# One held element's down projection moved from the end of the kernel into the next element's steps

## The chip, the core and the metric

The kernel runs on one core of a Trainium2 chip. The metric is the device time of one execution in microseconds (us); the median of three runs of the kernel before is 1217.96 us (1217.88 to 1219.26).

## The reference

A transformer block over x of 16 batch elements x 256 positions x 512 channels (f32): a WKV recurrence over the positions of each element, gated and added, then a feed-forward layer that is the sum of a routed part (8 experts, top 2, capacity 1280 rows, inner width 352) and a shared MLP (inner width 1408), gated and added.

```python
x = x + tanh(g_xattn[0]) * wkv(time_decay, time_first, layernorm(x), ctx_2048)
xf = layernorm(x).reshape(4096, 512)
gu = xf @ shared_w_up_gate                      # 512 x 2816
shared = (silu(gu[:, :1408]) * gu[:, 1408:]) @ shared_w_down      # 1408 x 512
logits = xf @ router                            # top 2 of 8, softmax of the two
h = silu(gate) * up                             # per expert, up to 1280 rows, 512 -> 2 x 352
routed = scatter_add(weight * (h @ w_down))     # 352 -> 512
x = x + tanh(g_ffn[0]) * (routed + shared)
```

## The kernel before

**Units and tiles.** One batch element is a unit (u, 0 to 15), made of two tiles of 128 rows (t, 0 and 1; tile number 2u + t). The array `acc` keeps the running sum x of the tiles in SBUF. Every engine has a program of its own, written out in order; semaphores with constant or counted values join them. Each unit is cut into 11 steps (s), one per block of 128 of the shared MLP's 1408 inner columns, and in each step each engine does its part of the MLP for this unit, plus stages of the recurrence and normalization for units to come, at places set by the table `STAGE_AT` (an offset of steps for each of a unit's two tiles). Of those, the stages `divide`, `turn_y`, `add_y`, `norm_x2`, `split_x` and `logits` follow each other from DVE over PE, DVE, ACT and DVE; `split_x` is followed by SyncE's transposing DMA into `xT` (L470), which the `logits` and the next unit's up projection read.

**The shared MLP in f16 halves.** Each f32 operand is split into a high and a low f16 part, and each product is three matmuls. In step s of unit u PE runs `up_pair` (L1060 to L1083), 24 matmuls of 256 columns into PSUM `PU`; ACT takes the silu and the high part, DVE the product (L1373), GpSimd (POOL) the low part (L690). The stages `logits` and `turn_y` are called in the middle of `up_pair`, behind its 9th and 18th matmul. Behind step s of unit u, PE runs `down_block(u - 1, s - 1)` (L1104 to L1116): for both tiles of the unit before, 3 matmuls of 512 columns each, into PSUM `PD[0]` and `PD[1]`, accumulated over the 11 blocks; the last step has two blocks. DVE adds the result into `acc` in step 0 of unit u + 1 (`add_down`, L1426 to L1429). SyncE then stores the finished tiles of units 0 to 12 into the DRAM array `moe_d` (`start_sums`).

**Held units.** Units 13, 14 and 15 (HELD = 3) get no down blocks in the steps: `if s > 0 and not (u.fixed and not 1 <= u.v <= FIRST_HELD)` (L1151), with FIRST_HELD = 13, stops them after unit 13's steps, which carry unit 12's blocks. Their hidden values stay in `hreg`, in three buffers. `held_down(u, t)` (L1214 to L1225) does one tile of a unit, a half, in one piece: 11 blocks x 3 = 33 matmuls of 512 columns. Half (13, 0) runs between unit 15 and the first expert, while the routed rows are gathered; the other five run behind the last expert.

**The experts.** 71 tiles of 128 routed rows (NPOS). For each, POOL gathers the rows from DRAM and SyncE transposes them; PE runs `expert_up` (24 matmuls of 352 columns), `turn_hidden` (3 transposes) and `expert_down` (9 matmuls of 512 columns into `PD[t % 2]`, L1202 to L1212); ACT, DVE and ACT again handle the hidden values and stage the output; POOL adds it into `moe_d` with an accumulating indirect DMA (L809).

**The end.** When the last of these has landed (`rows_added`), SyncE loads the routed sums of the held tiles, 1.5 MB, from `moe_d` (L576), starts two DRAM to DRAM copies of 3328 KB each, `moe_d` to the output, for units 0 to 12 (L578), and then stores the six held tiles from `acc`, 256 KB each (L583), each as soon as its down projection has been added and the routed sums of all six tiles are in (`combined`). DVE adds the six sums (L1626) and then the held halves that are left, in order:

```python
for c in range(FIRST_HELD * UT, TILES):
    sp.wait_ge(combined, HTILES)
    sp.wait_ge(down_added, c + 1)
    sp.dma_start(out_rows[c * P:(c + 1) * P, :], acc[:, c * D:(c + 1) * D]).then_inc(out_stored, 16)
```

Of the kernel before, what the change touches and what calls it, by code (L numbers as in the profile page):

```python
# [12 lines left out]
TILES = BATCH * STEPS // P  # L13
UNITS = BATCH
UT = STEPS // P
# [12 lines left out]
JT = J // P  # L28
# [5 lines left out]
NPOS = NTOK * TOPK // P + E - 1  # L34
# [16 lines left out]
HELD = 3  # L51
PE_TURNED = 2
SQ = 32
FIRST_HELD = UNITS - HELD
HTILES = HELD * UT
SP_N = 3
LOOP = (1, 6)
FIRST_AT = {
# [118 lines left out]
def build(nc, x, ctx_in, g_x, g_f, t_decay, t_first, router, w_ug, w_dn, s_ug, s_dn, out):  # L177
    es = ExitStack()
    with es:
# [118 lines left out]
        wst += [sUw[:, D * r:D * (r + 1)] for r in range(STAGED)]  # L298
        sums = sUw[:, STAGED * D:(STAGED + HTILES) * D].rearrange("p (j c) -> p j c", j=HTILES)

# [37 lines left out]
        PD = [pb(f"PD{r}", [P, 512]) for r in range(2)]  # L338
        PT = pb("PT", [P, 512])
        PR = pb("PR", [P, 512])  # L340
# [24 lines left out]
        down_ready = sem("down_ready"); down_added = sem("down_added")  # L365
# [33 lines left out]
        combined = sem("combined"); out_stored = sem("out_stored")  # L399
# [11 lines left out]
        EARLY_PARTS = 10 + len(ZERO_AT)  # L411
        assert (HTILES + 4) * P == len(ZERO_AT) * UN
        up_set = [(PU[0], PU[1]), (PU[2], PL)]

        def ring_of(u, m):

            n = JT * u.v + m
            if m >= SP_N:
                return n - SP_N + 1
            if u.fixed and u.v == 0:  # L420
                return None
            return JT * (u.v - 1) + max(q for q in range(JT) if q % SP_N == m) + 1

# [4 lines left out]
        def _(sp):  # L428
# [51 lines left out]
            def clear_rows(n):  # L480
                lo = NTOK - HTILES * P + n * UN
                sp.wait_ge(pmade, PMADE)
# [94 lines left out]
            for lo in range(0, held, held // 2):  # L577
                sp.dma_start(out_rows[lo:lo + held // 2, :].rearrange("(p a) d -> p (a d)", p=P),  # L578
                             moe_d[lo:lo + held // 2, :].rearrange("(p a) d -> p (a d)", p=P)).then_inc(out_stored, 16)
            for c in range(FIRST_HELD * UT, TILES):  # L580
                sp.wait_ge(combined, HTILES)
                sp.wait_ge(down_added, c + 1)
                sp.dma_start(out_rows[c * P:(c + 1) * P, :], acc[:, c * D:(c + 1) * D]).then_inc(out_stored, 16)  # L583
            sp.wait_ge(out_stored, 16 * (2 + HTILES))
            sp.wait_ge(moe_started, 16 * MOE_PARTS)
# [8 lines left out]
        def _(pool):  # L594
# [91 lines left out]
            def hidden_lo(u, m):  # L686
                n = JT * u.v + m
                r = m % SP_N
                pool.wait_ge(hhi_ready, n + 1)
# [129 lines left out]
        def _(act):  # L819
# [63 lines left out]
            def hidden_silu(u, m):  # L883
                n = JT * u.v + m
                r = m % SP_N
                act.wait_ge(up_ready, n + 1)
# [114 lines left out]
        def _(pe):  # L1001
# [99 lines left out]
                pe.matmul(PL[0:1, E:E + NPOS], home_of, Pm, start=True, stop=True).then_inc(homes_turned, 1)  # L1101
                pe.matmul(PL[0:1, E + NPOS:E + 2 * NPOS], one, Pm, start=True, stop=True).then_inc(homes_turned, 1)

            def down_block(u, j):  # L1104

                if u.fixed and u.v == 0:
                    pe.wait_ge(wd_lo, j + 1)
                elif j == 0:
                    pe.wait_ge(down_added, UT * u.v)
                pe.wait_ge(hlo_ready, JT * u.v + j + 1)  # L1110
                for t in range(UT):
                    for a, b in ((0, 0), (0, 1), (1, 0)):
                        mm = pe.matmul(PD[t][:, :], hh[:, u.par, j, a, t * P:(t + 1) * P], sD[:, j, b, :],  # L1113
                                       start=(j == 0 and a + b == 0), stop=(j == JT - 1 and a == 1))
                    if j == JT - 1:
                        mm.then_inc(down_ready, 1)  # L1116

            def unit(u, first=0):
                for s in range(first, JT):
                    for v, k in tiles_at("turn_k", u, s):  # L1120
                        if turned_by_pe(v):
                            turn_k(v, k)

                    def attend():
                        for v, k in tiles_at("turn_v", u, s):
                            if turned_by_pe(v):
                                turn_v(v, k)
                        for v, k in tiles_at("logits", u, s):
                            logits(v, k)
                        if u.fixed and u.v >= UNITS - 2:  # L1130
                            if s == (7 if u.v == UNITS - 2 else 1):
                                positions(LAST[u.par], TILES - 1 + u.par)
                            if u.v == UNITS - 1 and s == 3:
                                count_all()
                            if u.v == UNITS - 1 and s == 5:
                                place_homes()
                        elif u.par == 1 and s == 8 and not (u.fixed and u.v < 0):
                            positions(group_route(u.half), UT * u.v + 3)

                    def attend_late():  # L1140
                        for v, k in tiles_at("turn_y", u, s):
                            turn_y(v, k)

                    if u.fixed and u.v < 0:
                        attend()
                        attend_late()
                    else:
                        if u.fixed and u.v == UNITS - 1 and s == TABLE_AT:
                            turn_table()
                        up_pair(u, s, attend, attend_late)  # L1150
                    if s > 0 and not (u.fixed and not 1 <= u.v <= FIRST_HELD):  # L1151
                        down_block(u.shift(-1), s - 1)
                        if s == JT - 1:
                            down_block(u.shift(-1), s)

            pe.wait_ge(pmade, PMADE)
            pe.wait_ge(tab_in, 32)
# [43 lines left out]

            def expert_down(t, h):  # L1202
                pe.wait_ge(ehlo_ready, t + 1)
                if t >= 2:
                    pe.wait_ge(ostaged, t - 1)
                for m in range(IT):
                    M = IM[m]
                    for a, b in ((0, 0), (0, 1), (1, 0)):
                        mm = pe.matmul(PD[t % 2][:, :], ehT[0:M, t % 2, a, m * P:(m + 1) * P],  # L1209
                                       weights(h, UW + (m * 2 + b) * D, M, D),  # L1210
                                       start=(m == 0 and a + b == 0), stop=(m == IT - 1 and a == 1))
                mm.then_inc(edown_ready, 1)  # L1212

            def held_down(u, t):  # L1214

                PX = (PD, (PT, PR))[u % 2][t]
                if u == UNITS - 1:
                    pe.wait_ge(down_added, UT * (u - 2) + t + 1)
                buf = 2 if u == UNITS - 1 else u % 2
                pe.wait_ge(hlo_ready, JT * (u + 1))  # L1220
                for j in range(JT):
                    for a, b in ((0, 0), (0, 1), (1, 0)):
                        mm = pe.matmul(PX[:, :], hh[:, buf, j, a, t * P:(t + 1) * P], sD[:, j, b, :],  # L1223
                                       start=(j == 0 and a + b == 0), stop=(j == JT - 1 and a == 1))
                mm.then_inc(down_ready, 1)  # L1225

            pe.wait_ge(x2_done, TILES)
            held_down(FIRST_HELD, 0)
            pe.wait_ge(gidx_ready, 3)
            pe.wait_ge(down_added, FIRST_HELD * UT)  # L1230
            pe.wait_ge(homes_ready, 1)
# [7 lines left out]
                h = g  # L1239
            turn_hidden(NPOS - 1)  # L1240
            expert_down(NPOS - 1, h)
            held_down(FIRST_HELD, 1)
            for u in range(FIRST_HELD + 1, UNITS):
                if u % 2 == 0:
                    pe.wait_ge(ostaged, NPOS)
                for t in range(UT):
                    held_down(u, t)

# [2 lines left out]
        def _(dve):  # L1253
            def wait_alone(s, v):


                dve.wait_ge(s, v)
                dve.sem_inc(dve_waits, 1)
# [164 lines left out]
                                                  op0=ALU.subtract, op1=ALU.mult))  # L1423
                dve.tensor_tensor(homes, PL[0:1, E:E + NPOS], no_home, ALU.add).then_inc(homes_ready, 1)

            def add_down(c, t, PX):  # L1426
                dve.wait_ge(down_ready, c + 1)
                dve.scalar_tensor_tensor(out=acc_tile(c), in0=PX[t][:, :], scalar=gates[:, 0:1], in1=acc_tile(c),
                                         op0=ALU.mult, op1=ALU.add).then_inc(down_added, 1)  # L1429

# [179 lines left out]
                dve.tensor_tensor(ehT[:, t % 2, 1, :], PR[:, 0:IT * P], ehT[:, t % 2, 0, :], ALU.subtract).then_inc(ehlo_ready, 1)  # L1610

            for t in range(NPOS + 1):
                if t == 2:
                    add_down(FIRST_HELD * UT, 0, (PT, PR))
                if t >= 1:
                    expert_hidden(t - 1)
                    expert_lo(t - 1)
                for e, q in chunks_at(t):
                    weights_lo(e, q)

            add_down(FIRST_HELD * UT + 1, 1, (PT, PR))
            wait_alone(down_added, FIRST_HELD * UT + 2)
            dve.wait_ge(sums_in, 16)
            for t in range(HTILES):
                c = FIRST_HELD * UT + t
                dve.tensor_tensor(acc_tile(c), sums[:, t], acc_tile(c), ALU.add).then_inc(combined, 1)  # L1626
            dve.wait_ge(combined, HTILES)
            for c in range(FIRST_HELD * UT + 2, TILES):
                add_down(c, c % UT, (PD, (PT, PR))[c // UT % 2])


# [19 lines left out]
```

## Time and profile before

| | us |
|---|---|
| median of 3 runs | 1217.96 |
| lowest, highest run | 1217.88, 1219.26 |
| span of the profiled execution, first to last instruction | 1215.5 |
| PE busy | 1150.4 |
| DVE busy | 701.0 |
| POOL busy | 632.3 |
| ACT busy | 488.7 |

The profiled execution has no device time of its own among the times; its span is 2.5 us below the median of the runs, which is what lies around the first and last instruction. All times below are counted from the first instruction. PE is TensorE's matmul stream, and PEclk the clock granted to it, where 1.00 is 2.4 GHz and 0.50 is 1.2 GHz. A row of the timeline gives the start, the time from the first start to the last end, the engine, line and operation, and in brackets the idle time before it with what ended it.

### The profile page before, as it was taken

The page shows a single profiled execution, that of the slowest core. Times are in us where ns is not written, and L with a number is a line of the kernel's source. Part 1 is how long each engine was busy: PE and PEld are TensorE (multiplying, and loading weights), DVE is VectorE, ACT ScalarE, POOL GpSimd, SP SyncE. Part 2 cuts the span into 40 slices and gives each one's busy share as a digit, 9 for nine tenths or more (in the row PEclk, how much of TensorE's full clock was granted, in tenths as well). Part 3 has the DMA queues.
Part 4 walks back from the last instruction along what each step waited for, and adds up shares of the span by engine and source line. Part 5 has one row for each costly group of instructions (what it writes and reads, how often), then busy time and mean ns, then how long its engine had stood idle before and what let it go on. Part 6 is the DMA issues. An engine that isn't in the chain of part 4 may idle for free.

```text
span 1215.5 us, 26048 instructions
## 1 busy us (share of the span) xinstructions
PE 1150.4 (95%) x8284; PEld 803.5 (66%) x8284; DVE 701.0 (58%) x1385; ACT 488.7 (40%) x901; POOL 632.3 (52%) x754
## 2 busy tenths in 40 slices
PE   1489999999999999999999899999999999999998
PEld 1367777777777777777777677666666666666653
DVE  5878787787787787877878855322232222231112
ACT  5666453443443444435435243333343333333220
POOL 7889447456456456456466642444444444444320
PEclk9989999999999999999999999999999999999999
DMA  8554543333343333433443315999999898988748
GB/s 233 139 141 112 135 88 75 83 87 84 73 94 79 83 82 78 101 81 69 114 99 65 67 48 102 205 174 174 173 172 174 165 178 168 178 161 132 128 58 315
DMA packets 296006, 150.98 MB, mean 124 GB/s; under 512 B 236125, under 2 KB 260725, under 8 KB 295776
## 3 DMA queue, kind: packets, MB, share of 16 engines
q1 hardware_dynamic: 277024, 112.24, 40.5%
q0 software_dynamic: 18048, 37.47, 18.0%
q8 instruction: 51, 0.84, 0.3%
q14 instruction: 51, 0.42, 0.1%
q10 hardware_dynamic: 832, 0.02, 0.0%
HBM read 77.17 MB, written 52.31 MB: 107 GB/s over the span
## 4 chain that ended last, share of the span: by engine, by line
PE 77%; issue 7%; DVE 5%; POOL 3%; ACT 2%; DMA 1%; POOLq 1%; DVEq 0%; ACTq 0%; SPq 0%
PE PU L1080 31%; PE PD L1113 14%; PE PU L1188 12%; PE PD L1209 9%; PE PL L1188 4%; PE PR L1199 1%; PE PT L1004 1%; PE PR L1223 1%; PE PT L1223 1%; PE PD L1223 1%; DVE wkv L1338 1%; DMA moe_d<-wkv,acc 1%; POOL xT L792 1%; POOL slot_d L674 0%; POOLq L802 0%
## 5 line engine op out<-in xcount | busy, mean ns | idle before, releaser
L1080 PE MATMUL PU<-xT,wreg 128*128 128x256 f16 x4224 | 503.1, 276 | 1.9 <-DVE srng L1373 1.9
L1080 PEld LDWEIGHTS PU<-xT,wreg 128*128 128x128 f16 x4224 | 414.1, 99 | 81.7 <-issue 2.5
L809 POOL DMA_INDIRECT moe_d<-wkv,acc x71 | 112.0, 1578 | 215.9 <-ACT wkv L984 209.4
L1188 PE MATMUL PU<-acc,wkv 128*128 x1284 | 214.5, 312 | 0.0
L1113 PE MATMUL PD<-wreg,hreg 128*128 128x512 f16 x858 | 206.4, 379 | 0.0
L1188 PEld LDWEIGHTS PU<-acc,wkv 128*128 128x128 f16 x1284 | 125.2, 98 | 69.3
L1610 DVE TENSOR_TENSOR wkv<-PR,wkv 128x384 f16<-128x384 f32 x71 | 39.6, 557 | 208.0 <-ACT wkv L978 208.0
L1209 PE MATMUL PD<-acc,wkv 128*128 (+1 forms) x639 | 149.6, 379 | 1.5 <-DVE wkv L1610 1.5
L890 ACT ACTIVATE srng<-PU 128x256 f32<-128x256 f32 x176 | 66.8, 379 | 200.4 <-PE PU L1080 153.2
L690 POOL TENSOR_TENSOR hreg<-srng,hreg 128x256 f16<-128x256 f32 x165 | 120.0, 731 | 43.3 <-ACT hreg L906 42.4
L1113 PEld LDWEIGHTS PD<-wreg,hreg 128*128 128x128 f16 x858 | 83.9, 98 | 73.5
L906 ACT ACTIVATE hreg<-srng 128x256 f16<-128x256 f32 x176 | 72.3, 411 | 118.1 <-DVE srng L1373 118.0
L1373 DVE SCALAR_TENSOR_TENSOR srng<-PU,srng 128x256 f32<-128x256 f32 x176 | 73.3, 417 | 62.7 <-ACT srng L890 50.0
L1209 PEld LDWEIGHTS PD<-acc,wkv 128*128 128x128 f16 (+1 forms) x639 | 62.5, 98 | 67.7 <-issue 1.7
L1338 DVE RECIPROCAL wkv<-wkv 128x512 f32<-128x512 f32 x32 | 106.9, 3341 | 0.1
L984 ACT ACTIVATE wkv<-PD,acc 128x512 f32<-128x512 f32 x71 | 48.8, 687 | 106.5 <-PE PD L1209 82.8
L674 POOL DMA_INDIRECT slot_d<-stw,sidx x64 | 68.4, 1069 | 22.2 <-issue 15.5
L974 ACT ACTIVATE wkv<-PU 128x352 f32<-128x352 f32 x71 | 33.0, 465 | 113.3 <-PE PU L1188 61.6
L662 POOL TENSOR_TENSOR wkv<-wkv 128x512 f32<-128x512 f32 x32 | 38.7, 1209 | 69.6 <-DVE wkv L1314 69.5
L1188 PE MATMUL PL<-acc,wkv 128*128 x420 | 68.4, 313 | 0.0
L635 POOL TENSOR_SCALAR ve<-mv 128x1 f32<-128x1 f32 x64 | 14.4, 224 | 100.7 <-DVE mv L1288 97.4
L1004 PE MATMUL PT<-ident,wkv 128*128 128x128 f32 x144 | 26.2, 311 | 37.5 <-ACT wkv L854 26.3
(178 smaller groups left out, 1335.1 us busy)
## 6 DMA issues: line engine op xcount, KB each, us to landing
wreg<-in_L_ffn_w_up_gate SPq DMA_DIRECT2D x48, 176.0 KB, 3.9
acc<-in_x SPq DMA_DIRECT2D x32, 256.0 KB, 3.3
xhl_d<-wkv SPq DMA_DIRECT2D x32, 256.0 KB, 2.4
wkv<-in_ctx SPq DMA_DIRECT2D x112, 64.0 KB, 2.5
k_d<-wkv SPq DMA_DIRECT2D x28, 256.0 KB, 3.4
wkv<-k_d SPq DMA_DIRECT2D x112, 64.0 KB
moe_d<-acc SPq DMA_DIRECT2D x13, 512.0 KB
out<-moe_d SPq DMA_DIRECT2D x2, 3328.0 KB, 21.2
```

Of the source, the lines that this page charges most:

```text
L674: pool.indirect_dma_start(out=slot_d, out_offset=bass.IndirectOffsetOnAxis(ap=sidx[:, 2 * (r.at + t) + k:2 * (r.at + t) + k + 1], axis=0), ...
L690: pool.tensor_tensor(hh[:, u.par, m, 1, :], srng[:, r, :], hh[:, u.par, m, 0, :], ALU.subtract).then_inc(hlo_ready, 1)
L809: pool.indirect_dma_start(out=moe_d, out_offset=bass.IndirectOffsetOnAxis(ap=didx[:, t:t + 1], axis=0), in_=ostage[t % 3], in_offset=None, ...
L890: act.activation(srng[:, r, :], PU[r][:, 0:UN], ACT.Silu, scale=1.0 / WS).then_inc(silu_done, 1)
L906: act.activation(hh[:, buf, m, 0, :], srng[:, r, :], ACT.Copy).then_inc(hhi_ready, 1)
L984: act.activation(ostage[t % 3], PD[t % 2][:, :], ACT.Copy, scale=wslot[:, t:t + 1]).then_inc(ostaged, 1)
L1080: mm = pe.matmul(PU[r][:, gu * UN:(gu + 1) * UN], sU[:, m, gu, a, kt, :], xT[:, u.par, b, kt, :], start=(kt == 0 and a + b == 0), stop=(kt ...
L1113: mm = pe.matmul(PD[t][:, :], hh[:, u.par, j, a, t * P:(t + 1) * P], sD[:, j, b, :], start=(j == 0 and a + b == 0), stop=(j == JT - 1 and ...
L1188: mm = pe.matmul(up_set[t % 2][gu][:, 0:I], xgT[:, t % 4, a, kt, :], weights(h, ((gu * 2 + b) * KT + kt) * I, P, I), start=(kt == 0 and a ...
L1209: mm = pe.matmul(PD[t % 2][:, :], ehT[0:M, t % 2, a, m * P:(m + 1) * P], weights(h, UW + (m * 2 + b) * D, M, D), start=(m == 0 and a + b = ...
L1338: dve.reciprocal(nd[:, 1], nd[:, 1]).then_inc(rcp_done, 1)
L1373: dve.scalar_tensor_tensor(out=srng[:, r, :], in0=PU[r][:, UN:2 * UN], scalar=HS / WS, in1=srng[:, r, :], op0=ALU.mult, op1=ALU.mult).then ...
```

## The change

Unit 13's down projection runs block by block in unit 14's steps, as those of units 0 to 12 do in the units behind them, into both `PD` buffers. Half (14, 0) takes the place of (13, 0) between unit 15 and the first expert; halves (14, 1), (15, 0) and (15, 1) stay for the end, in `PR`, `PT` and `PD[1]`. DVE adds both tiles of unit 13 before the first expert's work, and the first `expert_down` waits for that. Semaphore counts are numbered by the new order, `HELD_ORDER`, and SyncE waits for `combined` once instead of for each store.

```diff
+EARLY_HALVES = (0, 1)
+FRONT = (UNITS - 2, 0)
+ENDING = ((UNITS - 2, 1), (UNITS - 1, 0), (UNITS - 1, 1))
+HELD_ORDER = tuple((UNITS - HELD, t) for t in EARLY_HALVES) + (FRONT,) + ENDING
...
-            for c in range(FIRST_HELD * UT, TILES):
-                sp.wait_ge(combined, HTILES)
-                sp.wait_ge(down_added, c + 1)
+            sp.wait_ge(combined, HTILES)
+            for n, (u, t) in enumerate(HELD_ORDER):
+                c = UT * u + t
+                sp.wait_ge(down_added, FIRST_HELD * UT + n + 1)
                 sp.dma_start(out_rows[c * P:(c + 1) * P, :], acc[:, c * D:(c + 1) * D]).then_inc(out_stored, 16)
...
-            def down_block(u, j):
+            def down_block(u, j, halves=range(UT)):
...
+                    if s > 0 and u.fixed and u.v == FIRST_HELD + 1:
+                        down_block(u.shift(-1), s - 1, EARLY_HALVES)
+                        if s == JT - 1:
+                            down_block(u.shift(-1), s, EARLY_HALVES)
...
             def expert_down(t, h):
                 pe.wait_ge(ehlo_ready, t + 1)
+                if t == 0:
+                    pe.wait_ge(down_added, FIRST_HELD * UT + UT)
...
             def held_down(u, t):
-                PX = (PD, (PT, PR))[u % 2][t]
-                if u == UNITS - 1:
-                    pe.wait_ge(down_added, UT * (u - 2) + t + 1)
+                PX = (PT, PR, PT, PD[1])[HELD_ORDER.index((u, t)) - UT]
+                if (u, t) == ENDING[1]:
+                    pe.wait_ge(down_added, FIRST_HELD * UT + UT + 1)
+                if (u, t) == ENDING[2]:
+                    pe.wait_ge(ostaged, NPOS - 1)
...
-            held_down(FIRST_HELD, 0)
+            held_down(*FRONT)
...
-            held_down(FIRST_HELD, 1)
-            for u in range(FIRST_HELD + 1, UNITS):
-                if u % 2 == 0:
-                    pe.wait_ge(ostaged, NPOS)
-                for t in range(UT):
-                    held_down(u, t)
+            for u, t in ENDING:
+                held_down(u, t)
...
             for t in range(NPOS + 1):
+                if t == 0:
+                    for k in range(UT):
+                        add_down(FIRST_HELD * UT + k, k, PD)
                 if t == 2:
-                    add_down(FIRST_HELD * UT, 0, (PT, PR))
+                    add_down(UT * FRONT[0] + FRONT[1], 0, (PT, PR), FIRST_HELD * UT + UT)
...
-            for c in range(FIRST_HELD * UT + 2, TILES):
-                add_down(c, c % UT, (PD, (PT, PR))[c // UT % 2])
+            for n, (u, t) in enumerate(ENDING):
+                add_down(UT * u + t, n, (PR, PT, PD[1]), FIRST_HELD * UT + UT + 1 + n)
```

The first place is PE's program in unit 14, from step 0 to the middle of step 5. L1080 (after the change L1085) is `up_pair`, L1004 (L1009) a transpose of `turn_y`, L1049 (L1054) the `logits`, L1118 a matmul of `down_block`. Before:

```order
L1080 MATMUL PU0<-xT,wreg 128x256 x18
L1004 MATMUL PT<-ident,wkv 128x128 x4
L1080 MATMUL PU0<-xT,wreg 128x256 x6
L1080 MATMUL PU1<-xT,wreg 128x256 x24
L1080 MATMUL PU2<-xT,wreg 128x256 x24
L1080 MATMUL PU0<-xT,wreg 128x256 x24
L1080 MATMUL PU1<-xT,wreg 128x256 x24
L1080 MATMUL PU2<-xT,wreg 128x256 x9
L1049 MATMUL PL<-rt_w,xT 128x16 x8
```

And of the change, the end of the same stretch, steps 3 and 4 and the first part of 5:

```order
L1085 MATMUL PU0<-xT,wreg 128x256 x24
L1118 MATMUL PD0<-wreg,hreg 128x512 x3
L1118 MATMUL PD1<-wreg,hreg 128x512 x3
L1085 MATMUL PU1<-xT,wreg 128x256 x24
L1118 MATMUL PD0<-wreg,hreg 128x512 x3
L1118 MATMUL PD1<-wreg,hreg 128x512 x3
L1085 MATMUL PU2<-xT,wreg 128x256 x9
L1054 MATMUL PL<-rt_w,xT 128x16 x8
```

Behind each of the steps 1 to 9 now stand six matmuls of 512 columns, and twelve behind step 10; four such blocks stand ahead of the `logits` of step 5.

The second place is the end of PE's program, behind the last `expert_down` (L1209, after the change L1220). Before, `held_down` is L1223:

```order
L1209 MATMUL PD0<-acc,wkv 128x512 x2
L1223 MATMUL PR<-wreg,hreg 128x512 x33
L1223 MATMUL PD0<-wreg,hreg 128x512 x33
L1223 MATMUL PD1<-wreg,hreg 128x512 x33
L1223 MATMUL PT<-wreg,hreg 128x512 x33
L1223 MATMUL PR<-wreg,hreg 128x512 x33
```

And of the change, where it is L1236:

```order
L1220 MATMUL PD0<-acc,wkv 128x512 x2
L1236 MATMUL PR<-wreg,hreg 128x512 x33
L1236 MATMUL PT<-wreg,hreg 128x512 x33
L1236 MATMUL PD1<-wreg,hreg 128x512 x33
```

66 matmuls have left the end. On SyncE, POOL and ACT no instruction changes its place; on DVE the adds of unit 13's tiles come before the first expert's instead of one behind the second expert and one behind the last.

## Rows read from the trace of the kernel before

**Rows 1.** The page, busy us and share of the span by engine.
```profile
PE 1150.4 (95%) x8284; PEld 803.5 (66%) x8284; DVE 701.0 (58%) x1385; ACT 488.7 (40%) x901; POOL 632.3 (52%) x754
```
**Rows 2.** The chain that ended last, its end: start us, us, what.
```profile
1174.41 2.12 PE PD L1209 x9
1176.53 7.12 PE PR L1223 x33
1183.65 14.24 PE PD L1223 x66
...
1212.18 0.75 DVE acc L1428
```
**Rows 3.** Windows of units 12, 14, 15: us, busy us, PEclk, DMA share, GB/s.
```profile
587.59:631.93 44.34, 44.34 (x355) 33.54 (x354) 37.99 (x77) 20.34 (x38) 24.23 (x34) 1.00 0.41 94
...
677.37:719.01 41.64, 33.83 (x291) 28.33 (x290) 31.66 (x70) 14.53 (x32) 21.89 (x29) 0.92 0.31 71
719.01:751.78 32.77, 30.70 (x279) 26.96 (x280) 20.18 (x78) 15.99 (x37) 12.05 (x13) 1.00 0.26 50
```
**Rows 4.** Timeline of PE in units 14 and 15, where it had waited.
```profile
680.35 0.66 PE L1004 MATMUL PT<-ident,wkv 128*128 128x128 f32 x4 [0.86 <-DVE wkv L1341]
...
692.32 1.16 PE L1080 MATMUL PU<-xT,wreg 128*128 128x256 f16 x9 [0.18 <-DVE srng L1373]
697.68 0.38 PE L1049 MATMUL PL<-rt_w,xT 128*128 128x16 f16 x8 [4.20 <-DMA xT<-wkv]
...
715.48 0.36 PE L1049 MATMUL PL<-rt_w,xT 128*128 128x16 f16 x8 [1.05 <-DMA xT<-wkv]
...
719.01 3.76 PE L1080 MATMUL PU<-xT,wreg 128*128 128x256 f16 x33 [1.52 <-DVE srng L1373]
...
735.53 0.28 PE L1101 MATMUL PL<-acc 80*1 80x71 f32 x2 [2.06 <-DVE acc L1409]
```
**Rows 5.** Windows, the stretch behind the 4.20 us gap; columns as in rows 3.
```profile
698.00:700.00 2.00, 2.00 (x13) 1.50 (x10) 1.82 (x5) 0.28 (x1) 1.53 (x3) 0.50 0.00 0
```
**Rows 6.** Timeline of DVE and SyncE's queue in unit 14, steps 0 to 4.
```profile
680.99 1.40 DVE L1428 SCALAR_TENSOR_TENSOR acc<-PD,gates,acc 128x512 f32<-128x512 f32 x2
...
692.18 1.01 DVE L1355 TENSOR_TENSOR wkv<-wkv 128x512 f16<-128x512 f32 x1
...
698.66 0.69 DVE L1341 TENSOR_TENSOR wkv<-wkv 128x512 f32<-128x512 f32 x1
...
693.36 1.24 SPq L470 DMA_TRANSPOSE xT<-wkv  x1
```
**Rows 7.** Timeline of SyncE's queue at the end, the load of the sums.
```profile
1182.06 0.39 SPq L576 DMA_DIRECT2D wreg<-moe_d  x1
```
**Rows 8.** Copies (L578), six stores (L583) and the fifth alone: issues, us to landing.
```profile
L578 SPq DMA_DIRECT2D out<-moe_d x2: 630/926/1221, 1182.5 to 1183.2; - x2
...
DMA to landing us min/median/max: 16.9/21.2/25.5
...
L583 SPq DMA_DIRECT2D out<-acc x6: 340/344/369, 1193.1 to 1213.0; - x6
...
DMA to landing us min/median/max: 2.0/14.4/16.7
...
1205.88 0.34 SPq L583 DMA_DIRECT2D out<-acc  x1
...
DMA to landing us min/median/max: 7.7/7.7/7.7
```
**Rows 9.** All DMA between 1182 and 1216 us.
```profile
DMA packets 1810, 9.99 MB, mean 294 GB/s; under 512 B 144, under 2 KB 144, under 8 KB 1680
```
**Rows 10.** Windows at the end; columns as in rows 3.
```profile
1186.00:1192.00 6.00, 6.00 (x30) 2.74 (x28) 2.68 (x5) 0.00 (x0) 0.00 (x0) 1.00 1.24 493
...
1212.00:1213.00 1.00, 0.14 (x1) 0.00 (x0) 0.75 (x1) 0.00 (x0) 0.00 (x0) 1.00 0.07 27
```
**Rows 11.** Timeline of DVE at the end, the six adds of the routed sums.
```profile
1189.32 3.70 DVE L1626 TENSOR_TENSOR acc<-wreg,acc 128x512 f32<-128x512 f32 x6 [4.88 <-DMA wreg<-moe_d]
```

More of the change, by code:

```diff
@@ L1110, in down_block @@
                 pe.wait_ge(hlo_ready, JT * u.v + j + 1)
-                for t in range(UT):
+                for t in halves:
                     for a, b in ((0, 0), (0, 1), (1, 0)):
@@ L1241, in _ @@
             expert_down(NPOS - 1, h)
-            held_down(FIRST_HELD, 1)
-            for u in range(FIRST_HELD + 1, UNITS):
-                if u % 2 == 0:
-                    pe.wait_ge(ostaged, NPOS)
-                for t in range(UT):
-                    held_down(u, t)
+            for u, t in ENDING:
+                held_down(u, t)
         @block.vector
@@ L1424, in place_experts, with add_down @@
                 dve.tensor_tensor(homes, PL[0:1, E:E + NPOS], no_home, ALU.add).then_inc(homes_ready, 1)
-            def add_down(c, t, PX):
-                dve.wait_ge(down_ready, c + 1)
+            def add_down(c, t, PX, n=None):
+                dve.wait_ge(down_ready, (c if n is None else n) + 1)
                 dve.scalar_tensor_tensor(out=acc_tile(c), in0=PX[t][:, :], scalar=gates[:, 0:1], in1=acc_tile(c),
@@ L1619, in _ @@
                     weights_lo(e, q)
-            add_down(FIRST_HELD * UT + 1, 1, (PT, PR))
-            wait_alone(down_added, FIRST_HELD * UT + 2)
+            wait_alone(down_added, FIRST_HELD * UT + UT + 1)
             dve.wait_ge(sums_in, 16)
```

## The prediction

> **What bounds the kernel now.** I read the page's busy line first: TensorE (PE) is busy 95% of the span, the next engine 58% [rows 1]. So the time is PE's work plus the gaps in it, unless something else ends last. The chain of waits says what ends last: after the last expert's down projection PE runs the five held halves back to back, a single one is 7.12 us and two are 14.24 us (33 and 66 matmuls, 0.216 us each), and the last DVE add starts at 1212.18 and takes 0.75 us [rows 2]. The span ends at 1215.5, so 2.6 us lie behind that add: the store of the last tile.
>
> Then I looked for the gaps that the moved matmuls could fill, with the windows of whole units. Unit 12, a full unit with down blocks, takes 44.34 us and PE is busy in all of it. Unit 14, which has no down blocks, takes 41.64 us with PE busy in 33.83 of them and a mean clock of 0.92. Unit 15 takes 32.77 us [rows 3]. PE's timeline names the gaps in unit 14: 0.86 us before turn_y in step 0, 0.18 us in step 5, 4.20 us before the logits of step 5, 1.05 us before those of step 10, and 1.52 us before unit 15's first matmul; unit 15 has one of 2.06 us before place_homes [rows 4]. Behind the 4.20 us gap the granted clock is 0.50 from 698 to 700 us, that is 1.2 instead of 2.4 GHz [rows 5]: the engine had stood still, and now pays twice per matmul for some time.
>
> Last I read the other chain of the tail, which isn't the one that ended last but runs close behind it. SyncE issues the load of the sums at 1182.06, when the last expert rows have landed, and the two large copies right behind it, at 1182.5 and 1183.2 [rows 7, 8]. The second copy lands 25.5 us after its issue, at 1208.7. The six stores of the held tiles are issued from 1193.1 on; the fifth, issued at 1205.88, lands only 7.7 us later, at 1213.6, and the sixth, issued at 1213.0 into empty queues, lands in 2.0 us, at 1215.0 [rows 8]. So the transfers behind the last expert are through at 1213.6, 31.5 us after 1182.1, and PE gives up its last tile at 1212.2: the two chains end within 1.5 us of each other. In the last us before 1213 the queues' share is 0.07, about one of 16 engines [rows 10], so 15 of them were done at about 1212.
>
> **The change, part by part.** (1) Unit 14 gets eleven down blocks of unit 13, 66 matmuls at 0.216 us = +14.24 us of PE work [rows 2], 1.295 us per block, one behind each of steps 1 to 9 and two behind step 10. What of it is filled? With blocks, unit 14 has the contents of unit 12, 44.34 us, plus the 0.86 us gap in step 0, which lies ahead of the first block and so stays, plus two small position matmuls: 45.3 us against 41.64 now, so +3.7 us, and 10.5 us of the 14.24 fill gaps. Three checks that the gaps do close. The logits of step 5 wait for tile 30 of xT, there at 697.68; PE reaches them now at 692.32 + 1.16 = 693.5 us, and with four blocks (5.2 us) ahead, at 698.3 to 698.6. The arrival doesn't move, since its chain is DVE's: split_x at 692.18, SyncE's transpose issued at 693.36, 4.3 us to land [rows 4, 6]; up_pair of step 2, which split_x's place in DVE's order depends on, is only 1.3 us later than now and DVE was that far behind. The margin is 0.6 us or more. The first block (13, 0) waits for the two adds of unit 12, done at 680.99 + 1.40 = 682.4; PE gets there at about 684. The turn_y of step 5 needs DVE's product, started at 698.66 and 0.69 us long [rows 6]; PE gets there at 699.5, so a tenth or two may be waited. Without the 4.20 us gap I expect no low clock behind it. The bounds: +0.6 us if the 0.86 and 2.06 us gaps go as well (45.3 less 0.9 less 2.1 less 41.64, about +0.7), and +14.24 if nothing is filled. I take +3.7, by the nearest row, unit 12's.
>
> What the low clock costs now is in the difference of the two windows: 41.64 less 30.1 (unit 12 without its blocks) leaves 11.5, of which 7.8 are gaps and 3.7 slow matmuls.
>
> (2) Unit 15 and the experts move later by the same 3.7 us. The route chain on DVE that makes the 2.06 us gap hangs on PE's own positions matmuls of step 1, so the gap stays. At the start one held half remains (now (14, 0), the same 33 matmuls). DVE's two adds of unit 13, 0.7 us each, come before the first expert's work, where DVE is idle three quarters of the time: nothing.
>
> (3) At the end PE has three halves instead of five: it starts them at 1176.53 + 3.7 = 1180.2 and ends at 1201.6. If that still set the end, the span would be 1201.6 + 0.75 + 2.6 = 1204.9, 10.6 us less.
>
> (4) But the expert rows land 3.7 us later, and everything behind them is unchanged in bytes: sums, two copies, six stores, 9.99 MB in the window [rows 9]. SyncE issues the sums at 1185.8. Sums are there 7.2 us later (1193.0; DVE's adds started at 1189.32 now), six adds of 3.7 us in all end at 1196.7, DVE's three held adds follow by 1202.4 [rows 11]. So all six stores are issued by 1203.2, while the copies fill the queues until 1212.4: stores queue behind them. The drain is now 31.5 us for five stores, and the sixth no longer comes into empty queues but as one more: 256 KB at between 294 GB/s (the mean) and 493 GB/s [rows 9, 10] is 0.53 to 0.89 us, I take 0.65. Last landing 1185.8 + 31.5 + 0.65 = 1217.9, and 0.5 us from landing to the end as now (1215.0 to 1215.5): 1218.4, **2.9 us more** than 1215.5. What was cover for the transfers, 14.2 us of PE work behind the last expert, is gone from there, and only 10.5 us came back in front. If the straggling queue of [rows 10] is chance, the drain is up to 1.1 us shorter: +1.8.
>
> The skill's figure speaks otherwise. The Trainium skill, "DMA: Bandwidth & Descriptors", section "Anatomy of one DMA — SWDGE (gpsimd) path", fits a DMA's time as 2.0 us plus its bytes at 436 GB/s (for the software path; these go through the hardware one). By that, 9.99 MB would be an estimated 24.9 us instead of 31.5 + 0.65, and the end 1211.2, 4.3 us less than now. The trace doesn't agree: 294 GB/s on average here.
>
> The sum is against the profiled execution's span; the median of the runs, 1217.96, is 2.5 us above it, and I add the same: **1220.9 us**. About 0.2%, 2.4 us, is what a measurement can tell from no change.
>
> **Rivals.** (a) The waits of unit 14 stay. If tile 30 comes later with PE's later steps, by some 1.3 us per block, PE waits again and the clock falls again: 4.2 us plus 3.7 us on top, 1228.8; half of that is 1224.9. For it: DVE's chain passes the hidden products that PE feeds. Against: DVE was the late one there. Chance 0.12.
> (b) The other side: the copies, not PE, set the end, but go faster than in this execution. At the 493 GB/s of 1186 to 1192 us [rows 10] 9.99 MB take 20.3 us, plus 1.9 us until data flow and 0.5: 1208.5 in span, 1211.0. It decides the sign from a drain shorter than 29.2 us on, 2.9 less than I take. The skill's rule above lands between, at about 1213.7. For it: the drain's mean is well under its best stretch. Against: nothing in it changes, and the second copy alone needs 25.5 us. Chance 0.06.
> (c) The change does just what it seems to: PE sets the end, -10.6 us, 1207.4. It needs a drain under 18.6 us. Chance 0.04.
> (d) The 0.86 and 2.06 us gaps go too: 2.9 us less than the forecast, no change, 1218.0. Chance 0.06.
>
> **How the numbers follow.** The forecast's case, the end set by transfers, has 0.72, from +1.4 to +5 us (1219.4 to 1223.0), centred at +2.6 with the straggler half counted; the bound of 2.4 us cuts it: 0.42 slower, 0.30 the same. Slower: 0.42 + 0.12 = 0.54. Same: 0.30 + 0.06 = 0.36. Faster: 0.06 + 0.04 = 0.10. The range leaves out the faster cases and the worst of (a): 1216.8 to 1225.0.
>
> **What would show it.** Unit 14 should last 45 us with no gap above 1 us and clock 1.00; the last expert's down projection should end 3.7 us later; three held halves should end near 1202, with PE idle for 15 us at the end; the chain of waits should end in the copies and stores, DMA where PE stood; the sums should be issued near 1186 and the last store land near 1218. I am wrong if the last DVE add is again within 3 us of the end, if a gap before the logits of step 5 is left, or if the time from the sums' issue to the end isn't 31 to 33 us.

## The result, and the profile after

The changed kernel takes 1220.3 us, median of 13 runs (1219.11 to 1221.68), against 1217.96 us for the kernel before, median of 13 as well (1216.88 to 1219.26). The ratio is 1.0018, with a 95% interval of 1.001 to 1.0025: slower by 2.3 us, just under the 0.2% that I had named as what can be told, and yet outside zero by its interval. The profiled execution has a span of 1217.9 us, where the kernel before had 1215.5. In every run whose span is on record the device time is 1.7 to 1.9 us above the span (here 1219.6 for 1217.9). The 2.5 us given ahead of the prediction for what lies around the span are therefore not that alone: some 0.7 us of them are what the profiled execution of the kernel before was quicker than the median of the runs.

The windows of units 14 and 15 of the changed kernel (us, then busy us of PE, its weight loads, DVE, ACT and POOL, then PEclk, DMA share, GB/s) answer to [rows 3]:

```profile
677.04:722.65 45.61, 44.75 (x357) 33.51 (x356) 33.16 (x79) 15.84 (x34) 23.42 (x32) 1.00 0.31 66
722.65:755.18 32.53, 30.58 (x281) 27.07 (x280) 18.63 (x71) 14.99 (x34) 10.51 (x11) 1.00 0.24 49
```

Unit 14 takes 45.61 us where it took 41.64, at full clock: of the 14.24 us of added matmuls, 10.3 us fill what stood empty or ran slowly. PE's timeline shows what happened to the gaps of [rows 4]:

```profile
680.03 0.66 PE L1009 MATMUL PT<-ident,wkv 128*128 128x128 f32 x4 [0.86 <-DVE wkv L1350]
...
696.84 1.15 PE L1085 MATMUL PU<-xT,wreg 128*128 128x256 f16 x9
697.82 0.35 PE L1054 MATMUL PL<-rt_w,xT 128*128 128x16 f16 x8
...
718.23 0.35 PE L1054 MATMUL PL<-rt_w,xT 128*128 128x16 f16 x8
...
738.92 0.28 PE L1106 MATMUL PL<-acc 80*1 80x71 f32 x2 [1.95 <-DVE acc L1418]
```

The logits of step 5 (697.82) and of step 10 (718.23) no longer wait. The gap of 0.86 us ahead of the first block and the one ahead of place_homes, now 1.95 us, are still there. DVE and SyncE's queue did the work that the logits of step 5 need at the same times as before, 0.3 us earlier like everything in this execution from unit 14 on [rows 6]:

```profile
691.85 1.01 DVE L1364 TENSOR_TENSOR wkv<-wkv 128x512 f16<-128x512 f32 x1
...
698.34 0.69 DVE L1350 TENSOR_TENSOR wkv<-wkv 128x512 f32<-128x512 f32 x1
...
693.02 1.24 SPq L474 DMA_TRANSPOSE xT<-wkv  x1
```

The end of the chain that ended last, as the chain view draws it, in start, us, what ([rows 2] are its like of before):

```profile
1177.81 2.12 PE PD L1220 x9
1179.93 7.12 PE PR L1236 x33
1187.05 7.12 PE PT L1236 x33
1194.17 7.14 PE PD L1236 x33
1201.31 0.03 issue
1201.34 0.75 DVE acc L1437
```

The view follows semaphores back from the last instruction that it counts, and it stops at 1202.09 in a span of 1217.9: it doesn't name what fills the last 16 us. SyncE's timeline and the landing times do (issue of the sums, of the two copies, of the six stores; then us from issue to landing of copies and of stores), as [rows 7, 8] did before:

```profile
1185.51 0.39 SPq L580 DMA_DIRECT2D wreg<-moe_d  x1
1185.94 1.92 SPq L582 DMA_DIRECT2D out<-moe_d  x2
1196.61 5.84 SPq L588 DMA_DIRECT2D out<-acc  x6
...
DMA to landing us min/median/max: 17.4/21.5/25.7
...
L588 SPq DMA_DIRECT2D out<-acc x6: 341/424/435, 1196.6 to 1202.1; - x6
...
DMA to landing us min/median/max: 15.4/16.8/17.3
```

The last store is issued at 1202.1, as soon as its tile is ready, and lands 15.4 us later, at 1217.5. In the kernel before the last store found the queues empty and landed in 2.0 us. That this store isn't slow but stands behind the copies is my reading here; e2, below, shows it.

### The profile page after: what moved, and what is told of

It is laid out like the page before. It is cut to its first block, busy times and chain, and to the rows that moved or that the text cites. A ratio compares the mean times of both kernels' runs of the same rounds, so it can differ in the third digit from the quotient of the medians.

```text
span 1217.9 us, 26044 instructions
## 1 busy us (share of the span) xinstructions
PE 1146.5 (94%) x8284; PEld 802.0 (66%) x8284; DVE 700.1 (57%) x1385; ACT 488.6 (40%) x901; POOL 631.8 (52%) x754
## 4 chain that ended last, share of the span: by engine, by line
PE 82%; DVE 6%; issue 3%; POOL 2%; ACT 2%; DMA 0%; DVEq 0%; POOLq 0%; ACTq 0%
PE PU L1085 30%; PE PU L1197 16%; PE PD L1118 14%; PE PD L1220 11%; PE PL L1197 5%; PE PR L1208 2%; DVE wkv L1347 1%; PE PT L1236 1%; PE PT L1009 1%; PE PD L1236 1%; PE PR L1236 1%; DVE srng L1382 1%; POOL slot_d L679 0%; POOL wreg L685 0%; DVE wkv L1364 0%
## 5 line engine op out<-in xcount | busy, mean ns | idle before, releaser
L1085 PE MATMUL PU<-xT,wreg 128*128 128x256 f16 x4224 | 501.5, 275 | 0.3 <-DVE srng L1382 0.2
L1085 PEld LDWEIGHTS PU<-xT,wreg 128*128 128x128 f16 x4224 | 412.9, 99 | 80.6 <-issue 0.8
L1118 PE MATMUL PD<-wreg,hreg 128*128 128x512 f16 x924 | 222.3, 379 | 0.0
L1220 PE MATMUL PD<-acc,wkv 128*128 (+1 forms) x639 | 149.6, 379 | 1.5 <-DVE wkv L1619 1.5
L1118 PEld LDWEIGHTS PD<-wreg,hreg 128*128 128x128 f16 x924 | 90.4, 98 | 79.2
L1220 PEld LDWEIGHTS PD<-acc,wkv 128*128 128x128 f16 (+1 forms) x639 | 62.5, 98 | 67.7 <-issue 1.7
L1009 PE MATMUL PT<-ident,wkv 128*128 128x128 f32 x144 | 25.8, 308 | 38.2 <-ACT wkv L859 25.2
```

What stands on the lines that cost most here:

```text
L1085: mm = pe.matmul(PU[r][:, gu * UN:(gu + 1) * UN], sU[:, m, gu, a, kt, :], xT[:, u.par, b, kt, :], start=(kt == 0 and a + b == 0), stop=(kt ...
```

## The experiments

Two theories stood at the start. T: the gaps in front give back only part of what moved, and what is behind the last expert is set by the transfers, not by PE. The rival with the most to say against it, R2: the blocks in unit 14 cost something by themselves. R1, that PE still sets the end, was already weak by the trace above.

### e1: one half in unit 14 instead of two

```diff
-EARLY_HALVES = (0, 1)
+EARLY_HALVES = (0,)
-ENDING = ((UNITS - 2, 1), (UNITS - 1, 0), (UNITS - 1, 1))
+ENDING = ((UNITS - 3, 1), (UNITS - 2, 1), (UNITS - 1, 0), (UNITS - 1, 1))
```

(with the semaphore counts that follow from it)

> Only half (13, 0) runs in unit 14's steps, four halves are left for the end. Theory T (the end is set by the transfers behind the last expert, about 32 us from the issue of the sums to the last landing, whatever PE does there): unit 14 needs 30.1 + 7.1 + 0.9 us plus a wait of about 1.8 us before the logits of step 5, about 40 us, so the sums are issued about 1.5 us earlier than in the kernel before (near 1180.6) and the span ends near 1213, 2.4 us below the kernel before: about 1215.6 us. Rival R1 (PE still sets the end): last DVE add near 1203, span near 1207, time near 1209.5. Rival R2 (the blocks in unit 14 themselves are what costs, in proportion): half of the 2.3 us lost, about 1219.1.

Measured: 1219.0 us, ratio to the kernel before 0.9998 (0.9989 to 1.0007). My number missed by 3.4 us, and the trace says where. Windows of units 14 and 15 of e1, then PE's timeline at the logits of step 5:

```profile
677.59:720.18 42.59, 39.33 (x324) 31.07 (x323) 32.14 (x72) 15.24 (x34) 22.56 (x30) 0.96 0.34 70
720.18:754.37 34.19, 32.24 (x280) 27.92 (x279) 19.63 (x77) 15.39 (x35) 11.36 (x12) 0.95 0.25 46
...
698.34 0.36 PE L1055 MATMUL PL<-rt_w,xT 128*128 128x16 f16 x8 [2.40 <-DMA xT<-wkv]
```

Four half blocks (three matmuls each) ahead of the logits leave a gap of 2.40 us, and the clock falls behind it, so the unit takes 42.6 us and not 40; it falls once more in unit 15 (34.19 us against 32.53), and the first expert waited 0.7 us for its rows. These three make 4.9 of the 5.1 us by which the sums were issued later than expected (1185.7 for 1180.6). The other half of the expectation held: 31.6 us from the issue of the sums (1185.69) to the end of the span, while the last DVE add was over by 1209.3. Transfers, not PE, ended it, and R1 with its 1209.5 us is out. The time itself is the one that R2 had given (1219.1) and not T's 1215.6. The trace explains it without R2, but e1 alone doesn't refute R2; e5 has to.

### e2 and e3: the two copies left out

```diff
-            for lo in range(0, held, held // 2):
-                sp.dma_start(out_rows[lo:lo + held // 2, :].rearrange("(p a) d -> p (a d)", p=P),
-                             moe_d[lo:lo + held // 2, :].rearrange("(p a) d -> p (a d)", p=P)).then_inc(out_stored, 16)
-            sp.wait_ge(out_stored, 16 * (2 + HTILES))
+            sp.wait_ge(out_stored, 16 * HTILES)
```

in the changed kernel (e2) and in the kernel before (e3).

> The changed kernel without the two DRAM to DRAM copies of units 0 to 12 (that part of the output stays unwritten). T: nothing but PE is left to set the end; last add at 1201.3 + 0.75, store, span 1204.8 instead of 1217.9, time about 1207.2. R2 or any other cost before the last expert: PE's end doesn't depend on the copies, but if something else than they held the end, the span stays above 1210.

> The kernel before without the same two copies. T: they were hidden behind the five held halves, so the span stays at 1215.5 and the time at 1218.0 within 0.5 us. If the transfers already held the end before, it falls by 1 us or more.

Measured: e2 1207.7 us, e3 1219.2 us, where the kernel before had 1219.0 on that chip. Ratios 0.9907 (0.9892 to 0.9922) and 1.0003 (0.9993 to 1.0012). In e2 the chain's last add comes when PE has finished, and the span (1206.3) ends 2.6 us behind it. That is 1.5 us over the 1204.8 expected: the clock fell in unit 15 of this execution, which costs 1.7 us (see the last section):

```profile
1195.80 7.14 PE PD L1233 x33
1202.94 0.02 issue
1202.96 0.75 DVE acc L1434
```

The six stores, us from issue to landing, of e2 (first row) and of e3 (second row), and e3's last DVE add:

```profile
DMA to landing us min/median/max: 2.1/2.5/2.7
...
DMA to landing us min/median/max: 2.0/2.3/4.0
...
1212.87 0.75 DVE L1425 SCALAR_TENSOR_TENSOR acc<-PR,gates,acc 128x512 f32<-128x512 f32 x1 [6.37 <-PE PR L1220]
```

Without the copies the same stores land in 2.5 us where they took 16.8. In e3 PE still gives up its last tile at 1212.87, and the span, 1216.2, ends 3.3 us behind the start of that add, as in the kernel before. So leaving out 6.8 MB of copies gains nothing in the kernel before, and 12.4 us in the changed one (against e4, which ran beside e2 and, as shown next, is the changed kernel over again). These two runs show T for the end.

### e4: the copies written as pieces of 8 KB

The view of both copies has `p=416` instead of `p=P`.

> The changed kernel with the same two copies cut into pieces of 8 KB instead of about 53 KB (view with p=416 instead of p=128). T: whatever the drain loses or gains, the span follows one for one. If smaller pieces share the 16 engines better (the last engine was over 1 us behind the others in the kernel before), the drain of 32.0 us falls to 27 to 31 us and the time by the same 1 to 5 us, to 1215 to 1219; if the copies are held by the memory's rate, nothing changes, 1220.3. R2: no change either way.

Measured: 1220.16 us, ratio 1.0012 (1.0003 to 1.0021); from the sums' issue at 1188.02 to the end 31.7 us. But the pieces didn't change. These are the transfers between the issue of the copies and the end, in the changed kernel (window 1186 to 1218) and in e4 (1188.5 to 1220):

```profile
DMA packets 1810, 9.99 MB, mean 312 GB/s; under 512 B 144, under 2 KB 144, under 8 KB 1680
...
DMA packets 1810, 9.99 MB, mean 317 GB/s; under 512 B 144, under 2 KB 144, under 8 KB 1680
```

Both have 1810 packets, 130 of them of 8 KB or more, where 832 pieces of 8 KB would have made some 700 packets more; in both traces the copies' 6.8 MB are 128 packets of 53 KB. Source and destination of each copy are one contiguous stretch in DRAM under either view, and what the edit changed didn't reach the transfers. So e4 tests nothing about pieces. It is a second measurement of the changed kernel, as e8 is a third, and the question that it was built for stays open.

### e8: the changed kernel again

> The changed kernel unchanged, on the same chip as the next two: 2 to 3 us over the kernel before (ratio 1.0016 to 1.0025) by every theory.

Measured: 1221.44 us (1218.74 to 1221.97), ratio 1.002 (1.0011 to 1.003), with the kernel before at 1218.83, as expected.

### e5: the fill cut to the size of the gaps

```diff
+FILL_AT = {1: [(0, 0), (1, 0)], 2: [(0, 1), (1, 1)], 3: [(0, 2), (1, 2)], 4: [(0, 3), (1, 3)], 5: [(0, 4), (1, 4)],
+           6: [(0, 5), (1, 5)], 7: [(0, 6)], 8: [(0, 7)], 9: [(0, 8)], 10: [(0, 9), (0, 10)]}
...
+                        for t, j in FILL_AT.get(s, ()):
+                            held_blocks(FIRST_HELD, t, PD[t], [j])
+                    if u.fixed and u.v == UNITS - 1 and s == 4:
+                        held_blocks(FIRST_HELD, 1, PD[1], [6, 7, 8])
...
-            held_down(*FRONT)
+            held_blocks(FIRST_HELD, 1, PD[1], [9, 10])
+            held_blocks(FIRST_HELD + 1, 0, PT, list(range(8)))
...
+            held_blocks(FIRST_HELD + 1, 0, PT, [8, 9, 10])
```

> The work that fills is cut to the size of the gaps: unit 14 gets 17 half blocks (0.65 us each) instead of 22, eight of them ahead of the logits of step 5 as in the changed kernel; three go into unit 15 ahead of place_homes, where 1.95 us are idle; two and the first eight of half (14, 0) stand ahead of the experts; the other three of (14, 0) and three halves are left for the end. T (gaps in front, transfers behind): unit 14 about 42.4 us, unit 15's gap gone, 0.6 us less ahead of the experts, so the sums are issued 3.9 us earlier than in the changed kernel, near 1181.6; the same 32.4 us behind them; time 3.9 us under the changed kernel and 1.5 us under the kernel before. PE ends 10 us before the transfers. Rival (the one half of the last batch cost a new stall of its own, so fewer blocks don't help): no better than the kernel before plus 0.5 us. Rival R1 (PE sets the end): 9 us less.

Measured: 1215.87 us, ratio 0.9979 (0.997 to 0.9988); e8 in the same comparison is at 1221.44, so it is 5.6 us under the changed kernel, where I had 3.9, and 3.0 us under the kernel before, where I had 1.5. Windows of unit 14, of unit 15 and of the stretch ahead of the experts, then PE's timeline at place_homes:

```profile
677.80:720.18 42.38, 41.52 (x342) 32.02 (x341) 31.92 (x71) 15.32 (x33) 22.40 (x30) 1.00 0.31 70
720.18:752.71 32.53, 32.52 (x290) 27.96 (x288) 19.87 (x78) 15.42 (x35) 11.60 (x13) 1.00 0.24 49
752.71:759.18 6.47, 6.47 (x32) 2.94 (x30) 3.88 (x8) 0.80 (x2) 2.93 (x4) 1.00 0.90 226
...
736.46 0.28 PE L1108 MATMUL PL<-acc 80*1 80x71 f32 x2
```

42.4, 32.5 and 6.5 us, each as worked out: five half blocks fewer, no gap ahead of place_homes although three half blocks more are in the same 32.53 us. Half blocks cost what they last and no more: five fewer are 3.23 us less in unit 14, 0.65 us each, which is against R2. The 1.7 us beyond the expectation would fit the clock, below: without the 1.95 us gap it has nothing to fall behind in unit 15. That isn't shown for the medians; the two profiled executions, e5's and e8's, have the clock at 1.00 in units 14 and 15 and differ by 3.0 us in span.

### e6: unit 13 not held at all

```diff
-HELD = 3
+HELD = 2
-ZERO_AT = {(1, 1): 0, (1, 4): 1, (1, 5): 2, (1, 6): 3, (1, 9): 4}
+ZERO_AT = {(1, 1): 0, (1, 4): 1, (1, 5): 2, (1, 6): 3}
...
             for q in range(WCH):
                 load_chunk(1, q)
+            start_sums(Unit(0, FIRST_HELD - 1))
```

(DVE adds unit 13's tiles in step 7 of unit 15; waits on `moe_started` that guard only the older parts ask for one part less.)

> The changed kernel, but unit 13 is no longer held at all: its tiles are added in unit 15 and go to moe_d under the experts like units 0 to 12, so sums are 1.05 MB instead of 1.57, stores 1.05 instead of 1.57, copies 7.34 instead of 6.82: 9.44 MB instead of 9.96 behind the last expert. T: the bytes behind the last expert set the end; 0.52 MB less at about 310 GB/s is 1.7 us less than the changed kernel, about 1218.6 where that has 1220.3. If the drain is a matter of latency and not of bytes, or the early adds and the early store delay the routing or the gathers: no gain, or 1 us more.

Measured: 1219.17 us, ratio 1.0003 (0.9994 to 1.0012), 2.3 us under e8 where 1.7 were expected. From the issue of the sums (1187.37) to the end it is 30.0 us.

### e7: both

> The fitted order of blocks (e5) and unit 13 no longer held (e6) together: the two gains are in different places, one ahead of the experts and one in the bytes behind them, so they add: e5's time less 1.5 to 2 us, about 1214.1 where the kernel before has 1218.8; sums issued near 1182, 30.0 us from there to the end, last DVE add near 1200, so PE still isn't the end. Rival: the store of unit 13 now runs among the first gathers and delays the first expert, or the end is PE's by then: no better than e5.

Measured: **1214.45 us**, ratio 0.9965 (0.9951 to 0.9978): 4.5 us under the kernel before, beating both, where about 1214.1 was expected. The three rows are its chain's end and SyncE's issue of the sums; the span is 1212.4:

```profile
1182.26 0.39 SPq L583 DMA_DIRECT2D wreg<-moe_d  x1
...
1185.70 14.26 PE PD L1132 x66
...
1199.98 0.75 DVE acc L1444
```

The table is what the tails of all profiled executions say (us; "tail" is span end less the issue of the sums):

| kernel | MB behind the experts | sums issued | last DVE add starts | span end | tail |
|---|---|---|---|---|---|
| before | 9.96 | 1182.1 | 1212.2 | 1215.5 | 33.4 |
| changed | 9.96 | 1185.5 | 1201.3 | 1217.9 | 32.4 |
| e1 | 9.96 | 1185.7 | 1208.5 | 1217.3 | 31.6 |
| e4 | 9.96 | 1188.0 | 1203.6 | 1219.7 | 31.7 |
| e8 | 9.96 | 1185.9 | 1201.5 | 1217.0 | 31.1 |
| e5 | 9.96 | 1182.6 | 1200.2 | 1214.0 | 31.4 |
| e6 | 9.44 | 1187.4 | 1202.9 | 1217.4 | 30.0 |
| e7 | 9.44 | 1182.3 | 1200.0 | 1212.4 | 30.1 |
| e9 (kernel before, idle work) | 9.96 | 1184.2 | 1214.1 | 1217.4 | 33.2 |
| e2 (no copies) | 3.15 | 1187.4 | 1203.0 | 1206.3 | 18.9 |
| e3 (kernel before, no copies) | 3.15 | 1182.8 | 1212.9 | 1216.2 | 33.4 |

In the five rows from "changed" to e5 the last DVE add starts anywhere from 15.6 to 22.8 us behind the issue of the sums, and the tail stays between 31.1 and 32.4 us. With 0.52 MB less (e6, e7) it is 30.0 and 30.1, on average 1.6 us shorter, by two executions against five that spread over 1.3. These two also have two stores fewer, so bytes and number of transfers aren't told apart. The rows of the kernel before (before, e3, e9) and e2 are of the other kind: they end 3.3 us behind the start of their last add, whatever the bytes.

### e9: work without use in the gap, in the kernel before

```diff
+                    if u.fixed and u.v == UNITS - 2 and s == 4:
+                        pe.wait_ge(down_added, UT * FIRST_HELD)
+                        for j in range(7):
+                            for a, b in ((0, 0), (0, 1), (1, 0)):
+                                pe.matmul(PD[0][:, :], hh[:, 1, j, a, 0:P], sD[:, j, b, :], start=True, stop=True)
```

> The kernel before with 21 matmuls of 512 columns (4.5 us) behind step 4 of unit 14 whose result nobody uses, ahead of the logits of step 5 where PE stood still for 4.2 us; the output is unchanged. They separate the wait from the clock that falls behind it. C (the 3.7 us of slow matmuls were on the path, as the prediction counted): unit 14 takes 38 us instead of 41.6, time 3 us less than the kernel before. T2 (unit 14's length was set by the arrival of both xT tiles, so the time won ahead of step 10 is waited for there, with a new gap of about 4 us before the logits of step 10, and the clock may fall there): unit 14 40.5 to 42.5 us, time within 1 us of the kernel before.

Measured: 1218.95 us where the kernel before had 1218.99, ratio 0.9997 (0.9988 to 1.0006). The window of its unit 14, and PE's timeline:

```profile
677.54:719.05 41.51, 36.64 (x312) 29.16 (x311) 31.68 (x70) 14.62 (x32) 21.89 (x29) 0.97 0.35 70
...
692.16 4.70 PE L1159 MATMUL PD<-wreg,hreg 128*128 128x512 f16 x21
...
698.43 0.36 PE L1049 MATMUL PL<-rt_w,xT 128*128 128x16 f16 x8 [0.59 <-DMA xT<-wkv]
...
715.52 0.36 PE L1049 MATMUL PL<-rt_w,xT 128*128 128x16 f16 x8 [2.68 <-DMA xT<-wkv]
715.73 2.83 PE L1080 MATMUL PU<-xT,wreg 128*128 128x256 f16 x15
719.05 4.08 PE L1080 MATMUL PU<-xT,wreg 128*128 128x256 f16 x33 [0.49 <-DVE srng L1378]
```

The gap in step 5 is nearly closed and the clock stayed up behind it, but unit 14 takes 41.51 us, as before: the logits of step 10 wait 2.68 us for the other tile of xT, and run at 715.52 where they ran at 715.48 in the kernel before. The slow matmuls behind the first gap were not on the path. Behind the new gap the clock fell instead (the 15 matmuls at 715.73 take 2.83 us, and 1.80 in the changed kernel), and that cost nothing either: the wait for DVE ahead of unit 15 went from 1.52 to 0.49 us, and unit 15 starts when it did.

## Why the prediction was right

The forecast was 1220.9 us for a measured 1220.3, its case was the right one, and the span was 1217.9 for 1218.4. The mechanism, gaps in front that give back less than the cover behind costs, is what the runs show. That the number fits to 0.6 us is in part luck: the drain was 0.7 to 1.3 us shorter in the other executions with the same bytes than in the profiled one of the changed kernel, and the low clock in unit 15 adds 1.7 us in some executions. The prediction counted the first as possible and didn't have the second, and they pull in opposite directions. Three executions of this program, the changed kernel's, e8's and e4's, have spans of 1217.9, 1217.0 and 1219.7 us. The 2.5 us from span to median hold an accident as well, as said with the result. Point by point:

- **Unit 14, +3.7 us.** It was 45.61 us for the 45.3 taken from unit 12, so +4.0, and 10.3 us filled for the 10.5 forecast. No gap before the logits of step 5, PE there at 697.82 (0.5 us before the time given, in an execution 0.3 us early); the 0.86 and 1.95 us gaps stayed, as said. The first held half of the end starts at 1179.93 against 1176.53, 3.4 us later, since unit 14 started 0.3 us earlier in this execution and unit 15 was 0.2 us shorter.
- **The end of PE, 1201.6.** It was 1201.3. PE then stands still for 16.6 us. The chain view didn't end in the copies and stores, as I had named among the signs: it stopped at the last DVE add, and the landing times had to be asked for.
- **The transfers.** Sums issued at 1185.5 for 1185.8, sums in use at 1192.88 for 1193.0, stores issued by 1202.5 for 1203.2, and 32.0 us from the first issue to the last landing (1217.5) for 32.15. The profiled execution is thus as long as the sum with the full straggler term; e1, e4, e8 and e5, at 31.1 to 31.7 us from the issue to the end of the span against 32.4, are nearer to the shorter drain that I had counted half. No run shows a cause for the difference among executions with the same transfers (32.4, 31.7, 31.1).
- **The rule of the Trainium skill, "DMA: Bandwidth & Descriptors", section "Anatomy of one DMA — SWDGE (gpsimd) path".** By that rule, which is fitted for the software path, 9.99 MB take an estimated 24.9 us. The window of the changed kernel's tail has 312 GB/s over 32.00 us, so the trace doesn't agree, and the measurement decides for the trace's rate, as the prediction had chosen:

```profile
1185.50:1217.50 32.00, 15.80 (x74) 6.96 (x71) 5.86 (x9) 0.00 (x0) 0.00 (x0) 0.80 0.91 312
```

- **Rivals.** (a) didn't occur: DVE's chain was the late one. (b) needed a drain under 29.2 us and (c) one under 18.6; it was 32.0. (d) didn't occur, but the two gaps that it needed weren't out of reach: e5 closed one of them.
- **What was wrong.** The sentence on what the low clock cost: "leaves 11.5, of which 7.8 are gaps and 3.7 slow matmuls". As arithmetic it holds, but the remainder is not what the clock cost. From the logits of step 5 (697.68 in the kernel before, 698.43 in e9) to the position matmuls (L1057, the rows below: before, then e9) PE took 8.68 us in the kernel before, most of it at the low clock, and 5.91 us in e9 at the full one. The low clock cost 2.8 us, not 3.7.

```profile
706.36 0.17 PE L1057 MATMUL PL<-ohs,pref 128*128 128x16 f16 x1
...
704.34 0.17 PE L1057 MATMUL PL<-ohs,pref 128*128 128x16 f16 x1
```

  And I took both parts for time to be won, while e9 shows that closing the first gap and keeping the clock wins nothing alone, since the next wait takes it back. What bounded unit 14 was the arrival of two tiles; the sum came out right since it was made from the length of a whole unit and not from the parts. The same error is in the expectation of e1, where half of the blocks were to bring most of the gain.
- **The spread of the runs** I hadn't foreseen either; the last section has it.

## What to carry to other kernels

When work is moved from the end of a kernel to gaps in front, ask first what it was covering: here five halves, 35.6 us of matmuls at the end, hid 31.5 us of transfers that can't start before the last expert. Cover that is longer than the transfers is worth moving only down to their length; the change took 14.2 us of it and got 10.3 us of gaps for them. Fill gaps up to their size and no further, by the arrival times of what each wait is for (17 half blocks and not 22, three of them in another gap); a block too many delays everything behind it one for one (0.65 us for each half block, e5). And if the last store takes 15 us to land where an undisturbed one takes 2, the end belongs to the queues, whatever the chain of waits names, and bytes are what to take out (0.52 MB, 1.6 us).

## What the runs showed of the hardware

- **Half clock behind the same gap, in some executions only.** The gap ahead of place_homes, 1.95 to 2.13 us long, is in nine of the eleven profiled executions. The clock falls behind it in six (e1, e2, e3, e4, e6, e9) and stays at 1.00 in three (before, changed, e8); the program of changed, e8 and e4 is the same. In e4 unit 15 takes 34.19 us instead of 32.53, 1.7 us more. The first two rows are e4's windows (unit 15, and the stretch behind the gap), the third is the changed kernel's window of the same place, and the last two are the 87 matmuls behind the gap, in e8 and in e4:

```profile
723.23:757.42 34.19, 32.24 (x281) 27.94 (x279) 18.61 (x71) 15.00 (x34) 10.52 (x11) 0.95 0.24 46
740.00:744.00 4.00, 4.00 (x24) 3.03 (x23) 1.62 (x6) 1.19 (x3) 0.62 (x1) 0.60 0.42 107
...
739.00:743.00 4.00, 4.00 (x39) 3.49 (x40) 2.28 (x6) 1.38 (x4) 0.62 (x1) 1.00 0.47 121
...
739.42 9.67 PE L1085 MATMUL PU<-xT,wreg 128*128 128x256 f16 x87
...
739.84 11.34 PE L1085 MATMUL PU<-xT,wreg 128*128 128x256 f16 x87
```

  So this gap costs its own length and, in six executions of nine, about as much again. Whether the spread of the runs comes from it isn't shown. Of the 13 runs of the changed kernel five are at 1219.1 to 1219.9, three at 1220.3 and five at 1221.2 to 1221.7, and 1.7 us is nearly the distance of the outer groups; but the mean clock of each run is on record and doesn't tell them apart (0.989 to 0.991 in both), since it takes in the low clock while PE stands still at the end as well (0.80 in the window of the changed kernel's tail). That e5's runs, without that gap, lie within 1.7 us (1215.08 to 1216.78) where e8's spread over 3.2 would fit.
- **Another view of a contiguous copy left its packets as they were.** With `p=416` in place of `p=P` the DRAM to DRAM copies still move in 128 packets of 53 KB (e4). Whether other pieces would be faster, and what holds the copies, the memory or the 16 engines, no run here tells.
